# A decoder layer on one core: TensorE's program of attention written out for all 32 heads in place of its loop over pairs of heads

## The reference

```
q, k, v = (proj(Wq), proj(Wk), proj(Wv))
scores = jnp.einsum('bhqd,bhkd->bhqk', q, k)
scores = scores + bias.transpose(2, 0, 1)[None]
attn = jax.nn.softmax(scores, axis=-1)
ctx = jnp.einsum('bhqk,bhkd->bhqd', attn, v)
```

## Time and profile before

| | |
|---|---|
| median of 3 runs | 3970.04 us |
| the profiled execution | 3972.34 us, its span 3970.6 us |
| PE busy | 3727.9 us, 94% of the span |
| POOL busy | 2681.1 us, 68% |
| DVE busy | 2466.4 us, 62% |
| ACT busy | 2004.6 us, 50% |
| mean granted clock of TensorE | 0.977 of full speed |

### The profile page before, as it was taken

One profiled execution on the slowest core, in us unless ns is written; L12 is line 12 of the kernel. 1 busy time (PEld: TensorE's weight loads), 2 busy tenths in 40 slices (PEclk: granted clock), 3 DMA queues, 4 the chain that ended last, 5 costly groups with the idle time before them and its releaser, 6 DMA issues. The chain is left out here.

```text
span 3970.6 us, 64135 instructions
## 1 busy us (share of the span) xinstructions
PE 3727.9 (94%) x21277; PEld 2216.2 (56%) x21277; DVE 2466.4 (62%) x3356; ACT 2004.6 (50%) x3452; POOL 2681.1 (68%) x1402
## 2 busy tenths in 40 slices
PE   8989999999999989999999999999997999997899
PEld 7754444444444444444444444444446888885377
DVE  3466666666666656666666666666635777775632
ACT  3335555555555555555555555555553555553232
POOL 1128888888888878888988888889893343430010
PEclk9989999999999999999999999999998999998999
DMA  7652222432223452222332222332312333335710
GB/s 221 162 120 63 66 64 71 103 75 69 64 64 81 101 153 64 69 64 67 93 90 66 68 64 67 98 84 65 105 36 88 100 106 103 104 116 174 262 46 22
DMA packets 368370, 366.99 MB, mean 92 GB/s; under 512 B 189339, under 2 KB 261531, under 8 KB 362776
## 3 DMA queue, kind: packets, MB, share of 16 engines
q1 hardware_dynamic: 299064, 336.50, 31.6%
q10 hardware_dynamic: 67168, 20.98, 2.2%
q0 software_dynamic: 1920, 6.29, 0.5%
HBM read 142.64 MB, written 89.70 MB: 59 GB/s over the span
## 5 line engine op out<-in xcount | busy, mean ns | idle before, releaser
L354 POOL TENSOR_TENSOR acc<-acc,probs 128x1024 f32<-128x1024 f32 x894 | 2126.4, 2379 | 306.9 <-ACT probs L814 189.3
L939 DVE TENSOR_REDUCE maxes<-ps 128x2 f32<-128x1024 f32 x1024 | 1253.2, 1225 | 607.6 <-PE ps L610 596.7
L817 ACT ACTIVATE probs<-ps,far_bias 128x1024 f32<-128x1024 f32 (+7 forms) x1280 | 997.4, 819 | 795.4 <-DVE near_s L956 546.0
L641 PE MATMUL ps<-probs,v_head 128*64 128x512 f32 x4096 | 1002.1, 610 | 8.9 <-ACT ctx_out L800 6.9
L629 PE MATMUL ps<-stacks 64*128 64x512 f32 x6144 | 825.7, 398 | 1.8 <-ACT probs L814 1.8
L629 PEld LDWEIGHTS ps<-stacks 64*128 64x128 f32 x6144 | 591.0, 188 | 126.9 <-ACT probs L814 7.9
L610 PE MATMUL ps<-stacks 64*128 64x512 f32 x2048 | 508.0, 494 | 142.4 <-DVE maxes L939 56.9
L610 PEld LDWEIGHTS ps<-stacks 64*128 64x128 f32 x2048 | 194.5, 187 | 700.0 <-DVE maxes L939 464.3
L641 PEld LDWEIGHTS ps<-probs,v_head 128*64 128x64 f32 x4096 | 251.0, 137 | 463.0 <-issue 450.9
L956 DVE TENSOR_TENSOR near_s<-ps,near_bias 128x384 f32<-128x384 f32 (+2 forms) x576 | 265.8, 491 | 58.4 <-PE ps L629 55.3
L962 DVE TENSOR_TENSOR c_q<-ps,c_q 64x512 fp32r<-64x512 f32 x128 | 87.5, 684 | 311.2 <-ACT c_q L773 311.2
(11 more groups left out here) (278 smaller groups left out, 4515.4 us busy)
## 6 DMA issues: line engine op xcount, KB each, us to landing
stacks<-c_q SPq DMA_DIRECT2D x128, 256.0 KB, 4.3
stacks<-c_d SPq DMA_DIRECT2D x64, 512.0 KB, 6.9
stacks<-c_k SPq DMA_DIRECT2D x32, 768.0 KB, 5.5
stacks<-c_k SPq DMA_DIRECT2D x64, 384.0 KB, 7.0
scr_v<-probs ACTq DMA_DIRECT2D x32, 512.0 KB, 4.1
v_head<-scr_v SPq DMA_DIRECT2D x32, 512.0 KB, 8.5
scr_ctx<-ctx_out SPq DMA_DIRECT2D x128, 128.0 KB, 2.3
both_ctx<-scr_ctx SPq DMA_DIRECT2D x32, 512.0 KB, 4.0
```

What stands on the lines that cost most here:

```text
L354: pool.tensor_tensor(acc[:, qb, :], acc[:, qb, :], pr, ALU.add).then_inc(s["summed"], 1)
L641: mm = pe.matmul(ps[64 * half:64 * half + 64, PV, :], v_head[:, side, kt, :], probs[:, st % PT_RING, half * 512:(half + 1) * 512], start=k ...
L817: ins = act.activation(probs[:, st % PT_RING, a:z], sc[:, a:z], ACT.Exp, bias=bias)
L939: dve.tensor_reduce(maxes[:, qt:qt + HALF_GROUPS // 2 + 1:HALF_GROUPS // 2, first_chunk + pair], ps[:, bank:bank + 2, :], AX.X, ALU.max).t ...
```

## The change

PE alone no longer calls `heads`. Its program is generated by a plain loop at build time, so all 32 heads are written out one after the other; DVE, ACT, POOL and SP keep their loops. The semaphores and every count that they are compared with are the same.

```
-            heads(pe, head)
+            for n in range(-2, NH):
+                head(n, n // 2, n % 2)
             pe.wait_ge(s["exped"], NH * STEPS)
```

## The result

The changed kernel takes 4006.01 us (median of 4 runs, 4002.93 to 4011.86) against 3970.53 us (four runs now): a ratio of 1.0092, 95% interval 1.0075 to 1.011. It is 35 us slower, where no measurable change was forecast and 3981 us was the upper end. The profiled execution took 4004.79 us, its span 4003.0 us.

A forecast was written before the change was run, and what follows sets the result against it. The PE, busy 94% of the span, was taken as the bound. 8.5 us gained against 6.8 given back, or whole heads' 2.4 us more, gave 3970.04 + 2.4 = 3972.4 us, no measurable change (chance 0.68); range 3957 to 3981 us.

The forecast's parts named there:

- The branches go: Start of odd heads: without the loop's branch the PE starts 1.64 us earlier, 13 times, 21.3 us on paper.
- The keys and the clock take it back: After odd heads' starts: longer key waits and unhidden clock falls consume the time gained; 2.4 us more in sum.
- seams: The 13 places where the PE's loop branches back between heads; PE stands still 2.05 us at each, 26.7 us in all.
- The register arithmetic: Loop arithmetic on the PE's sequencer: hidden by queued matmuls, costed at nothing, at most 3 us if bare.
- fall of the clock: PE's granted clock drops to 1.2 of 2.4 GHz for 3.4 us after standstills; unhidden, 0.85 us a head.
- More program: Instruction fetch of the written-out PE program: 4 blocks a head against 4.4 in the loop; nothing added, no traffic.
- The rival on late fetches: PE's sequencer runs out of program at each block: 250 us at worst, 4220 us; chance 0.03.
- wait for keys: At g = 3, PE waits for the DMA of the next head's keys: 47.9 us, forecast to reach 65 to 75.
- the seams' share: Key wait at g = 3 in odd heads, forecast to grow 1.2 to 2.1 us, 13 times, once the branches go.
- The clock in every head: Rival: every head's full key wait brings a clock drop, 12.7 us more, 3982.7 us; chance 0.13.

The follow-up runs named there:

- e5: The kernel before, PE's program still a loop but with its branch announced by a back-edge hint, so the branch stall goes: 3976.09 us, ratio 1.0008.
- e6: The kernel before, with SP's four DMAs for the queries of head n + 2 issued ahead of the context store: 3915.94 us, ratio 0.9861.
- e7: The changed kernel, with SP's four DMAs for the queries of head n + 2 issued ahead of the context store: 3883.13 us, ratio 0.9776.
- e1: The changed kernel with 26 do-nothing instructions at the start of the PE's program, shifting all block borders: 4008.59 us, ratio 1.0088.
- e3: The changed kernel with heads padded to 1024 instructions and 91 more do-nothing instructions at the start of the PE's program: 4036.19 us, ratio 1.0154.
- e2: The changed kernel with 102 do-nothing instructions in each of heads 1 to 28, making a head 1024 instructions, four blocks: 3986.85 us, ratio 1.0035.
- e4: The kernel before, with its loop, and 125 do-nothing instructions at the start of the PE's program: 4047.79 us, ratio 1.0196.

## Why the prediction was wrong

- *The branches go, 21.3 us on paper.* Right. The waits at the heads' starts in heads 1 to 28 fell from 26.7 us and 15 times 0.41 to 28 times 0.41 us, 32.9 to 11.6 us.
- *The keys and the clock take it back, +2.4 us.* Right, as far as seams go. e5, which removes them and leaves the PE's program a loop, has 4.8 us more in heads 1 to 28 (2388.37 against 2383.54) and no difference in time. e6 and e7 show the reason from the other side: with SP's fill earlier, the seams' time and the clock's part come out as a gain of 33 us.
- *The register arithmetic, nothing.* Heads 3 and 8 of the changed kernel, which had no fall of the clock, are busy 79.95 and 79.99 us, beside 80.0 to 80.1 in the loop. Right.
- **The step that failed is "More program", where it says "Nothing added, and no traffic either".** There is indeed no more traffic: 124 packets in heads 1 to 28 before and 100 now, 3.6 a head. What was not asked is when they are fetched. Head 29 was taken as the proof that a written-out head costs nothing; its fetches lie elsewhere, those of head 30 in the changed kernel lie in the fill. The rival on late fetches looked for the harm in the wrong place: it priced the PE running out of program, which no wait of the written-out heads shows, and not the keys' DMA, which lands late when a block comes during the fill. Against 47.9 us, the wait for keys is 23.8 us longer by the seams' share (e5) and another 23.8 us beyond e5. Of these, 16.9 us are in heads 5, 10, 15, 20 and 25 (2.8 to 4.3 us each). In heads 2, 7, 12 and 17, whose fetch falls just ahead of the fill, 2.9 us in, it is 0.7 to 0.9 us each. Head 14 has 1.5 us and the other heads together 2.5 us, for which no run shows a cause. In whole heads 1 to 28 the changed kernel takes 30.3 us more than e5 (2418.63 against 2388.37), so some 30 of the 35 us come with the failed step, and some 5 us are the seams' share that the prediction did forecast.
- *The clock in every head* was half right as a rival: 23 heads of 1 to 28 have a fall instead of 17, and in the five heads with the long wait it lasts 6.8 us instead of 3.4. It makes 7.1 of the 35 us, as a consequence of the waits: with the waits for keys gone, in e7, one fall is left.
- Head 27 (87.68 us) is a small case of its own. Its long wait is on ACT, for the store of the context, with a block fetched 2.1 us before it ended; that the fetch is the cause was not tried:

```profile
2642.03 0.59 ACT L801 COPY ctx_out<-ps 128x512 f32<-128x512 f32 x1 [4.25 <-DMA scr_ctx<-ctx_out]
```

The Trainium skill, in Runtime: NRT & Kernel Launch, section Instruction fetch mechanics, says that crossing into the next block is mostly hidden and that kernels prefer full unrolling where possible. The trace agrees that the PE itself does not wait for a block. The runs disagree with the advice for this kernel as it stands: a block's transfer in the fill makes other transfers late, some 30 of the 35 us. With the earlier fill (e7) the advice holds, 33 us less than the loop with its seams.

## What to carry to other kernels

A program is data too: it is fetched by DMA, in blocks, at moments that the program's length sets. Before code is written out or made longer ahead of a loop, look where the instruction queue's packets fall against the transfer that someone waits for, and compare a few heads or passes, not one. And a standstill that is removed is worth something only if the wait behind it doesn't take the time back: here the same edit cost 35 us or gave 33 us, by four DMAs of SP standing ahead of or behind two stores.

## What the runs showed of the hardware

- The wait for keys by the place of a fetch of 16 KB in the head, in heads 1 to 28 without a seam and without head 14, of the two kernels and e1 to e5. With no fetch in the first 24 us it is 1.7 to 2.6 us.

| fetch, us into the head | wait for keys, us |
|---|---|
| 1.0 to 1.3 | 2.1 to 2.6 |
| 2.8 to 3.0 | 2.8 to 3.2 |
| 6.0 | 3.8 |
| 6.8 to 7.4 | 5.0 to 5.5 |
| 9.0 to 10.5 | 4.8 to 6.5 |
| 11.2 | 5.6 |
| 13.7 to 15.6 | 2.7 to 4.4 |
| 21 to 24 | 1.8 to 2.7 |

- 91 or 125 instructions that do nothing, run once at the start, moved the whole kernel by 49 us (e3, beside e2) and 74 us (e4). Ahead of head 1 stand 6.8 and 4.2 us of it; the rest came from where the blocks then began.
- A loop whose branch is announced was not fetched again after its first pass. A pass is 1955 instructions in the trace, 7.6 blocks; without the announcement the PE's queue moved 110 blocks between 600 and 2700 us, and in e5 there is no row of it left in the same stretch. DMA queues, the kernel before and then e5:

```profile
q1 hardware_dynamic: 142312, 164.95, 31.9%
q8 instruction: 110, 1.80, 0.3%
```

```profile
q1 hardware_dynamic: 142389, 164.85, 31.8%
q14 instruction: 3, 0.02, 0.0%
```
